# Two feed-forwards with routed experts: VectorE's pieces in another order, waits moved to the products that need them, weight stores moved

## What is computed

```python
x = x + 0.5 * _L0_ffn_ref(_layernorm(x, axis=-1), ...)
x = x + _L0_attn_ref(_layernorm(x, axis=-1), W_q, W_k, W_v, W_o)
x = x + 0.5 * _L0_ffn_ref(_layernorm(x, axis=-1), ...)
```

```python
def _swiglu(x, w1, w2, w3):
    return jax.nn.silu(x @ w1) * (x @ w2) @ w3
shared_out = _swiglu(x, shared_w1, shared_w2, shared_w3)      # hidden 1024
scores = jax.nn.sigmoid(x @ router_w)
_, top_idx = jax.lax.top_k(scores + expert_bias, 2)           # of 16 experts
acc + _swiglu(xf, w1, w2, w3) * g[:, None]                    # per expert, hidden 256
```

## Time and profile before

| | |
|---|---|
| median of 3 runs | 1635.55 us (1625.62 to 1637.22) |
| the profiled execution | 1634.56 us, span 1632.9 us |
| mean granted TensorE clock | 0.951 |
| TensorE busy | 1488.1 us, 91% |
| VectorE busy | 968.9 us, 59% |
| ScalarE busy | 649.4 us, 40% |
| first feed-forward, from the first up on | 60 to 590 us: chunks to 286, blocks 287 to 512, chunks behind from 516 |
| second feed-forward | from 1119 us: blocks from 1312, chunks behind from 1525 |

### The profile page before, as it was taken

How to read it: one execution, slowest core, us unless ns; L and a number is a source line. 1 busy time by engine, 2 the same in 40 slices (tenths; PEclk the granted TensorE clock), 3 DMA queues, 4 the chain that set the end, 5 groups by cost and what they waited for, 6 DMA issues and landing times. The chain is left out here.

```text
span 1632.9 us, 29065 instructions
## 1 busy us (share of the span) xinstructions
PE 1488.1 (91%) x9028; PEld 1207.0 (74%) x9028; DVE 968.9 (59%) x2051; ACT 649.4 (40%) x1302; POOL 599.7 (37%) x831
## 2 busy tenths in 40 slices
PE   5998999999988948999999999866999999999998
PEld 5877888888777835666666666535878888888787
DVE  5478865555544756676566566514766455555466
ACT  2323444343323213665555555524222334433232
POOL 5428820234322033464455354223288123333100
PEclk9999999999989978999999999966999999999999
DMA  9777974444596744354444444225087343447751
GB/s 312 259 274 253 326 257 144 153 141 143 190 362 241 245 146 107 84 129 121 127 120 106 112 115 115 80 76 181 33 326 275 114 162 116 134 143 251 227 184 52
DMA packets 176229, 283.17 MB, mean 173 GB/s; under 512 B 20691, under 2 KB 125651, under 8 KB 176099
## 3 DMA queue, kind: packets, MB, share of 16 engines
q1 hardware_dynamic: 135106, 204.87, 39.5%
q0 software_dynamic: 19104, 56.64, 9.4%
q10 hardware_dynamic: 21888, 19.93, 3.9%
HBM read 142.63 MB, written 108.79 MB: 154 GB/s over the span
## 5 line engine op out<-in xcount | busy, mean ns | idle before, releaser
L1216 PE MATMUL f_bank<-f_xparts,f_sw 128*128 128x512 f32 x1536 | 386.6, 402 | 17.5 <-DVE f_sw L1146 10.3
L1216 PEld LDWEIGHTS f_bank<-f_xparts,f_sw 128*128 128x128 f32 x1536 | 289.7, 195 | 75.3 <-issue 16.9
L831 POOL DMA_INDIRECT outputs_by_choice<-f_yr,f_home x160 | 153.9, 962 | 407.7 <-DVE f_yr L1173 335.5
L1861 DVE TENSOR_REDUCE at_mx<-at_ps 128x1 f32<-128x384 f32 (+3 forms) x352 | 215.1, 633 | 143.6 <-PE at_ps L2001 143.2
L1774 ACT ACTIVATE at_pT<-at_ps 128x512 f32<-128x512 f32 (+1 forms) x352 | 194.6, 560 | 91.8 <-PE at_ps L2017 81.7
L1691 POOL TENSOR_SCALAR_AFFINE_SELECT at_pT<-at_pT 128x128 f32<-128x128 f32 (+2 forms) x352 | 124.4, 361 | 251.4 <-ACT at_pT L1774 247.9
L2017 PE MATMUL at_ps<-at_qT,at_kT 98*128 98x256 f32 (+3 forms) x512 | 175.1, 395 | 21.0 <-DMA at_qT<-at_mT 19.3
L1299 PE MATMUL f_bank<-f_whi,f_hparts 128*128 x640 | 192.1, 422 | 0.1
L799 POOL DMA_INDIRECT rows_by_slot<-f_xq,slot x128 | 146.4, 1144 | 118.1 <-DVEq L985 79.7
L873 ACT CAST f_hparts<-f_hid 128x512 fp32r<-128x512 f32 x128 | 79.5, 621 | 256.3 <-DVE f_hid L1085 241.2
L1162 DVE TENSOR_TENSOR f_sil<-f_sil,f_bank 128x256 f32<-128x256 f32 x160 | 67.4, 421 | 171.2 <-ACT f_sil L889 165.2
(11 more groups left out here) (177 smaller groups left out, 2363.2 us busy)
## 6 DMA issues: line engine op xcount, KB each, us to landing
f_ring<-weights_in_parts SPq DMA_DIRECT2D x32, 768.0 KB
weights_in_parts<-f_whi SPq DMA_DIRECT2D x30, 768.0 KB, 3.8
f_rawx<-rows_by_slot ACTq DMA_DIRECT2D x152, 128.0 KB
f_ew<-outputs_by_choice SPq DMA_DIRECT2D x16, 1024.0 KB, 6.1
f_whi<-weights_in_parts SPq DMA_DIRECT2D x16, 768.0 KB
f_ew<-in_L_ffn_routed_w_dram SPq DMA_DIRECT2D x42, 256.0 KB
rows_by_slot<-zero POOLq DMA_DIRECT2D x10, 1024.0 KB, 21.5
f_xq<-xn_rows POOLq DMA_DIRECT2D x32, 256.0 KB
```

The lines of the kernel that those rows point to most:

```text
L831: nc.gpsimd.indirect_dma_start(dram.yk, bass.IndirectOffsetOnAxis(ap=home[:, i:i + 1], axis=0), yr[:, i % 4, :], None).then_inc(y_st[i % 4 ...
L1216: ins = pe.matmul(ps[j % 2][:, :], sw12[:, wp, k, w, j * P:(j + 1) * P], xparts[:, u, xp, k, :], start=(i == 0), stop=(i == 3 * KD - 1))
L1861: v.tensor_reduce(own, ps1[i % RING1][:, 0:heads * w].rearrange("p (j a x) -> p j a x", a=min(heads, 2), x=w), AX.X, ALU.max).then_inc(mx_ ...
```

## The change

- VectorE, in a step: the low part of the hidden values comes after all pieces but combine. The residual comes first among the pieces.
- The last residual before the blocks comes behind the first low part of rows.
- TensorE: rank stands behind up(5) and ahead of down(4) (before: behind down(3) of step 4); invert one step later, behind that step's up and ahead of its down.
- At the entry into the blocks the first transpose comes ahead of the last down, waiting for hid; the wait for the last residual moves to the down of block 0, in step 2 of the blocks. At the exit the wait for the last copy of y moves behind the second up, ahead of the first down.
- SP: the high weights of two experts are stored after each of the loads 4 to 11, so that all 16 are out by then; before one after each of the loads 4 to 15, and four at the end.
- In the first feed-forward two combines share steps 10 and 12 of the chunks behind instead of 13 and 14.

```diff
-                if not exact:
-                    store_high(e - RING)
+                if not exact and e < RING + E // 2:
+                    for i in range(2):
+                        store_high(2 * (e - RING) + i)
             low_in(E - 1)
             if not exact:
-                for e in range(E - RING, E):
-                    store_high(e)
                 sp.wait_ge(hi_st, 16 * E)
@@ VectorE, chunk
                     v.tensor_tensor(hid[:, j % 2], sil[:, j % 2, :], psB[j % 2][:, :], ALU.mult).then_inc(h_done, 1)
-                    dve.wait_ge(h_hi, n + 1)
-                    v.tensor_tensor(hparts[:, j % 2, 1], hid[:, j % 2], hparts[:, j % 2, 0], ALU.subtract
-                                    ).then_inc(h_lo, 1)
+                    if j == 0 and not fresh:
+                        residual(c - 1)
                     if not exact and n in PART_AT:
                         low_part(PART_AT.index(n), 0)
-                    if j == 0 and not fresh:
-                        residual(c - 1)
                     if j == 3 and not last:
                         low_x(1 - u, c + 1)
...
                     if n == INVERT_AT + 2 * PARTS + 2:
                         homes()
+                    dve.wait_ge(h_hi, n + 1)
+                    v.tensor_tensor(hparts[:, j % 2, 1], hid[:, j % 2], hparts[:, j % 2, 0], ALU.subtract
+                                    ).then_inc(h_lo, 1)
...
-                COMBINE_AT = [2, 3, 4, 5, 6, 7, 8, 9, 10, 11, 12, 13, 13, 14, 14, 15]
+                COMBINE_AT = [2, 3, 4, 5, 6, 7, 8, 9, 10, 10, 11, 12, 12, 13, 14, 15]
...
-            residual(BEHIND - 1)
...
             low_rows(0, 0)
+            residual(BEHIND - 1)
             steps(dve, step)
@@ TensorE, chunk
                     up(c, u, j, fresh)
+                    if c == 0 and j == 5:
+                        rank()
+                    part = c * z.JS + j - INVERT_AT - 2
+                    if part >= 0 and part % 2 == 0 and part // 2 < PARTS:
+                        invert(part // 2)
+                    if c == BEHIND and j == 1:
+
+                        pe.wait_ge(y_done, NB + 2)
                     if j > 0:
                         down(c, j - 1, fresh)
                     elif not fresh:
                         down(c - 1, z.JS - 1, False)
-                    if c == 0 and j == 4:
-                        rank()
-                    part = c * z.JS + j - INVERT_AT - 1
-                    if part >= 0 and part % 2 == 0 and part // 2 < PARTS:
-                        invert(part // 2)
@@ TensorE, passages
-            down(BEHIND - 1, z.JS - 1, False)
-            pe.wait_ge(sh_done, BEHIND * CT + 4)
-            if exact:
-                pe.wait_ge(ew_in, 16 * E)
-            else:
-                pe.wait_ge(hi_made, 2 * E)
...
                     pe.wait_ge(y_done, i - 1)
+                    if isinstance(i, int) and i == 2:
+
+                        pe.wait_ge(sh_done, BEHIND * CT + 4)
...
+            pe.wait_ge(h_done, BEHIND * z.JS + 1)
             turn_x(0, 0)
+            down(BEHIND - 1, z.JS - 1, False)
+            if exact:
+                pe.wait_ge(ew_in, 16 * E)
+            else:
+                pe.wait_ge(hi_made, 2 * E)
             steps(pe, step, True)
             pe.wait_ge(xT_lo, NB)
             pe.wait_ge(hT_lo, NB)
             pe.wait_ge(rh_done, NB + 2)
-            pe.wait_ge(y_done, NB + 2)
             chunks_behind(pe, chunk)
```

## The result

| | before | after |
|---|---|---|
| median, 20 runs each | 1634.54 us (1625.62 to 1638.01, and one of 7944.15) | 1623.15 us (1618.04 to 1629.18) |
| the profiled execution | 1634.56 us, span 1632.9 us | 1618.04 us, span 1616.3 us |
| mean granted TensorE clock | 0.951 | 0.959 |
| TensorE busy | 1488.1 us | 1475.9 us |

The ratio of the two is 0.9937, 95% interval 0.9923 to 0.9951: 10.3 us gained where 27.9 were forecast, and 2 us above the range's upper end of 1621. The profiled execution of after is the lowest of its 20 while that of before is at its median, so the spans of the two traces lie 16.6 us apart; 6 us of that are not of the change.

The account below looks back on a forecast made before the run. TensorE was taken as the bound (91% of the span), losing time in waits and the lower clock after them. Gains of 14.4 and 13.5 us, together 27.9 off 1634.56, gave 1606.7, left at 1606.5; range 1596 to 1621.

Parts of the forecast that it names:

- parts 1 to 3: Feed-forward steps with pieces ahead of the low part (17.1 us), entry into the blocks (4.3, 3.9), exit (6.0, 4.0).
- Rank: TensorE's rank, one up later, finds its input: 3.0 us gained in the first feed-forward, -0.4 in the second.
- entries: Into the blocks: transpose ahead of the last down, residual wait moved to block 2; 4.3 us gained in first feed-forward, 3.9 second.
- exit: Out of the blocks: wait for the last copy of y moved ahead of the first down; 6.0 and 4.0 us gained.
- first marks: Invert behind the next up on TensorE finds its marks ready: 4.4 us gained in each feed-forward.
- The residual's 1.6 us: Residual first among VectorE's pieces: the wait for it at the first feed-forward's fourth chunk goes, 1.6 us gained.
- Part 1, pieces ahead of the low part: VectorE runs pieces while ScalarE casts: 0.69 us back in every step with pieces; gains of the whole part 17.1 us.
- Part 1, block_experts: At step 10, block_experts ahead of the low part: a new TensorE stall of 1.85 us that pays back nothing.
- Part 4, combines: Chunks behind the first feed-forward's blocks: doubled combines earlier, 2.3 us gained; 1 us on VectorE, with 2.7 of slack.
- Part 5, stores: First feed-forward's blocks: more stores between loads delay the weights, -9.7 us; bounds 0 and 19 us of cost.
- rival A: Stores in the blocks hidden, as loads pass them or TensorE's waits hang on loads alone: 1597 us, chance 0.15.
- Rival B: Low parts too late: TensorE stops at each marks step, low clock follows; up to 1623.5 us, chance 0.15.

Follow-up runs that it names:

- e9_waits_alone: Kernel before with only the moved waits, including the new places of rank, invert and residual; ratio 0.982 to the kernel before.
- a0_again: The changed kernel, unedited, run a second time; ratio 0.9943 to the kernel before.
- e4_low_first_all: Changed kernel with VectorE's low part ahead of the pieces in every step, all else new; ratio 0.9892 to the kernel before.
- e1_stores_spread: Changed kernel with one high part stored per load and four at the end, as before the change; ratio 0.9923 to the kernel before.

## Why the prediction was wrong

**The mechanism of the moved waits (parts 1 to 3): right.** Rank 3.0 for 3.0, entries 4.2 for 4.3, exit 6.7 for 6.0, and the whole second feed-forward of e9_waits_alone 13.6 for 13.5 (its terms differ by up to 0.9: rank 0.5 for -0.4, first marks 3.6 for 4.4). The residual's 1.6 us are there in e9_waits_alone (2.2) and hidden by the stop in after.

**Part 1, pieces ahead of the low part: wrongly credited.** The text gives each step with pieces 0.69 us back. The waits for ScalarE's cast did mostly vanish, from 22.7 us in 33 waits to 4.8 in 7 in the same stretch. But VectorE set the pace in few steps only: the order alone is worth some 1.7 us at the later marks of the first feed-forward and nothing in the second, and from up(6) to up(14) it costs 0.2 us (a0_again) to 1.7 (after), where e4_low_first_all and e9_waits_alone lose none. The gain of the first marks belongs to the place of invert, since e4_low_first_all has 3.8 us of it with the old order.

**Part 1, block_experts: mis-sized.** "This stall is new and pays back nothing": 1.91 us as forecast, with up to 1.6 us of low clock behind it, which the same text describes elsewhere and did not add.

**Part 4, combines: the wrong sign,** 2.3 forecast, -4.3 measured. The text saw the load behind the store and took it for "1 us on VectorE, with 2.7 of slack". VectorE waited 1.01, 1.52 and 3.50 us, each on top of the combines of its step, and TensorE then 1.03 and 2.71 us for the hidden tile: there was no slack left. The forecast laid SP's chain of store and load over the new steps for one chunk, not for all three. And the 2.1 us which the old steps also lose show that a lead at the ups is no lead at the stage's end, when the last combines set it.

**Part 5, stores: right, slightly too dear,** -7.5 for -9.7, nearly all of it given back by e1_stores_spread; rival A, stores hidden, is out. The prediction took five more transfers at the 350 GB/s of the earlier trace rows, 11.2 us. Counted from the load that ends the long expert 2, the low part of expert 12 was in after 46.8 us, where before it was in after 38.9: 7.9 us. The DMA engines moved more while they were full, 405 GB/s from 434 to 474 us. Of the 1.50 us wait for rows that was to be given back, 1.0 us was still there. The Trainium skill (DMA: Bandwidth & Descriptors, Queues, rings and completion order) has the descriptors of a ring consumed in order. The trace agrees as far as it goes: the load of expert 7 took 11.5 us behind two stores, 9.6 behind one and 5.5 behind none. With the engines full, a sharing of the bytes alone would delay it too, and no run here tells the two apart.

**What no part had: the stop.** -5.0 in the second feed-forward and, against e9_waits_alone, -3.5 in the first. It stood in the trace of before at 215.82 and 1272.01 us and cost little there; a forecast that walks the timeline past it should have asked what a TensorE 8 us further ahead does when ScalarE and VectorE stand until a given moment. Whether it could have been priced stays open: no row of before shows TensorE losing by it in the second feed-forward, and it is missing on one chip.

Together: 14.4 - 2.5 (block_experts and first marks) + 0.8 (other marks) - 2.9 (residual and stop) + 2.2 (stores) + 0.6 (in and out) - 6.6 (behind) = 6.0 in the first; 13.5 - 1.0 (ahead of and at the first marks) + 0.3 (other marks) - 5.0 (stop) + 0.5 (in, blocks, out) = 8.3 in the second. The rest, to the 10.3 us of the runs, is the attention and the spread between executions, 4 us that no term explains. The two largest shortfalls are thus the stop and the combines: 7.9 and 6.6 us. Rival B, low parts too late at each marks step, did not happen (0.50 us at the first marks, 0.30 in the second feed-forward); of the 8.4 us that TensorE waits for low parts, 3.6 are at block_experts (1.91 and 1.71) and 2.3 at the first low product of the second feed-forward. The 0.5 us of stall forecast at rank came out at 0.47.

## What to carry to other kernels

Moving a wait from in front of a batch of work to the product that needs it did what the rows said; judge it apart from every reordering that comes with it. A transfer with no due time (a store for later) belongs into a stretch in which the queue is idle, found by looking at when each expert's blocks run, not at counts of experts: 12 us here, more than the whole change gave. A consumer moved to an earlier step helps only if its loads also come earlier, as the combines show.

## What the runs showed of the hardware

- ScalarE and VectorE stood idle up to 8.06 us at a time near the end of GpSimd's last indirect scatter, the last 3.5 to 3.8 us of it, in after, behind the modelled end of the up that ScalarE reads; in the first feed-forward TensorE's signals for the two halves of that up came 0.07 us apart at the end of it. The end of it moved from 213.65 to 158.94 us when half of the scatter was left out. In after ScalarE resumed 1.5 us behind the last scatter's end in the first feed-forward and VectorE 2.0 us in the second, where ScalarE had resumed 0.2 us before that end. The three traces without it are those of one chip.
- A stall of TensorE of 1.9 us was followed by twelve products at 4.50 us (granted clock 0.62) in one execution and not in another of the same kernel (2.91, granted clock 1.00).
- A load of 768 KB on SP's queue took 11.5 us with two stores of the same size ahead of it, 9.6 with one and 5.5 with none; TensorE's waits for such loads in the blocks were 15.1, 7.8 and 2.6 us. In the stretch of the waits the DMA engines were full in the first two cases (share 1.00 and 405 GB/s, 0.97 and 350 GB/s) and not in the third (0.74 and 251 GB/s).
